# The aggregation's weights and lane numbers are read from PSUM instead of SBUF

## The chip, the cores and the metric

The kernel runs on one core of a Trainium2 chip. The metric is the device time of one execution in microseconds (us). A difference in a row of the profile is in us too, unless it is marked ns. The engines are TensorE (PE; its weight loads are listed as PEld), VectorE (DVE), ScalarE (ACT), GpSimd (POOL) and SyncE (SP).

## What is computed

A graph layer over 2500 nodes with 512 channels and 40000 edges sorted by destination, followed by a token-mixing branch and a gated MLP. Two attention layers over the edges come first, and they hold the part that is changed:

```python
for l in range(L):                                   # L = 2
    q = (x @ Wq[l] + bq[l]).reshape(N, H, D)         # N = 2500, H = 8, D = 64
    k = (x @ Wk[l] + bk[l]).reshape(N, H, D)
    v = (x @ Wv[l] + bv[l]).reshape(N, H, D)
    a = (q[dst] * k[src]).sum(-1) * scale
    ...                                              # softmax of a over the edges of one dst
    agg = jax.ops.segment_sum(alpha[:, :, None] * v[src], dst, num_segments=N).reshape(N, C)
    x = agg + (x @ Ws[l] + bs[l]) + enc
```

The changed stage is the `segment_sum`: for each edge the row `v[src]` is fetched, multiplied by the edge's eight head weights, and added into the row of its destination node.

## The kernel before

The edges lie in 336 slots of 128 (SLOTS; one edge per partition). Each slot belongs to one tile of 128 destination nodes. Each layer runs, one block after the other with a barrier between them: `project_nodes` (q, k, v), `score_edges`, `soften` (the softmax), `aggregate` and `combine`. Nothing of one block overlaps the next.

`score_edges` and `aggregate` both fetch rows with `gather` (L761): GpSimd issues one indirect DMA per slot, 128 rows of 2 KB, into a ring of U = 16 buffers. Before gather s it waits until VectorE has used the buffer of slot s - 16. GpSimd does nothing else in either block.

In `aggregate` VectorE works per slot, in this order: the one-hot `hot` (L1068), which compares the row of lane numbers `T["lane"]` (0 to 127, 128x128 f32) with the edge's local node number, a per-partition scalar; every fourth slot the copy of four slots' weights into the last eight columns of `wv` (L1075); then it waits for the slot's rows to land and writes the product `wv = vbuf * wt` (L1078), with the eight weights spread over 64 channels each. `wt` holds the weights of eight slots, copied from `weights` by the staging instruction (L1056) every eight slots. `wv` is a ring of R = 8 slots and `hot` one of 16. Before the rings come round VectorE waits for TensorE (`summed`).

TensorE multiplies `hot` by `wv` into the accumulator `psA` (L1118): two f32 matmuls per slot, 256 and 264 columns, which stand in the trace as four matmul records. Every four slots its queue loads the numbers of the node tiles (L767). ScalarE moves a full accumulator to `agg` (L1093) and clears it (L1095), 20 times per layer. SP loads `x` from `base_rows`, 20 transfers of 256 KB per layer.

In `score_edges` the corresponding product (L829) is `psQ[i] * kbuf[u]`: one operand comes from PSUM and the other from SBUF. Its one-hots (L808) are bf16, from SBUF to SBUF. Each slot's gather is of the same size as in `aggregate`.

Of the kernel before, what the change touches and what calls it, by code (L numbers as in the profile page):

```python
# [14 lines left out]
P = 128  # L15
# [3 lines left out]
H = 8  # L19
# [12 lines left out]
U = 16  # L32
# [60 lines left out]
def one(ap):  # L93

    return ap.rearrange("p o c -> p (o c)")
# [10 lines left out]
def turns(engine, n, body):  # L106


    body(0)
    with engine.Fori(1, n) as t:  # L110
        body(t)
# [10 lines left out]
def later(t):  # L122

    return not isinstance(t, int) or t > 0
# [629 lines left out]
def gather(pool, T, bufs, table, landed, freed, started):  # L754

    for s in range(SLOTS):
        if s >= U:

            pool.wait_ge(freed, s - U + 1)
            pool.sem_inc(started, 1)  # L760
        pool.indirect_dma_start(bufs[:, s % U, :], None, table,  # L761
                                bass.IndirectOffsetOnAxis(ap=T["src"][:, s:s + 1], axis=0)).then_inc(landed[s % U], 16)


def node_tiles(nc, engine, T, slot, n):

    return nc.values_load_multi_w_load_instructions(T["tile_of"][0:1, bass.ds(slot, n)], engines=[engine.engine],  # L767
                                                    min_val=0, max_val=NT - 1)[1]
# [243 lines left out]
def aggregate(nc, a, T, layer, v_dram, weights, agg, base_dram, x):  # L1012

    with ExitStack() as stack:
        m = Memory(nc, stack, f"agg{layer}")
        h, B, R = U // 2, 4, 8
        vbuf = m.sb("vbuf", [P, U, C])
        hot = m.sb("hot", [P, U, P])  # L1020
        wt = m.sb("wt", [P, 2, h, H])
        wv = m.sb("wv", [P, R, AW])
        zeros = m.sb("zeros", [P, 2, C // 2 + H])
        psA = m.ps("psA", [P, 2, 2, C])
        landed = [m.sem(f"landed{u}") for u in range(U)]
        hots, staged, beside, weighted, summed, blank, evicted, kept, started = (
            m.sem(x) for x in ("hots", "staged", "beside", "weighted", "summed", "blank", "evicted",
                               "kept", "started"))
        base_in = m.sem("base_in")
        local = T["local"]  # L1030
        parts = ((0, C // 2), (C // 2, AW))
        with nc.Block() as block:
            @block.sync
            def _(sp):
                def tile(t):
                    if later(t):

                        sp.wait_ge(weighted, t * U)
                    sp.dma_start(one(x[:, bass.ds(t, 1), :]), base_dram[bass.ds(t * P, P), :]).then_inc(base_in, 16)
                turns(sp, NT, tile)  # L1040
                sp.wait_ge(base_in, 16 * NT)

            @block.gpsimd
            def _(pool):
                gather(pool, T, vbuf, v_dram, landed, weighted, started)

            @block.vector
            def _(vec):
                vec.memset(zeros[:], 0.0).then_inc(blank, 1)

                def stage(t, half):
                    if later(t):

                        vec.wait_ge(weighted, (t - 1) * U + half * h + h)
                        vec.wait_ge(beside, (t - 1) * (U // B) + (half * h + h) // B)
                    vec.tensor_scalar(wt[:, half].rearrange("p u h -> p (u h)"),  # L1056
                                      weights[:, bass.ds((t * U + half * h) * H, h * H)],
                                      1.0, None, ALU.mult).then_inc(staged, 1)
                    vec.wait_ge(staged, t * 2 + half + 1)

                def turn(t):
                    for u in range(U):
                        if u % h == 0:
                            stage(t, u // h)
                        if later(t):

                            vec.wait_ge(summed, t * U + u + 2 - U)
                        vec.tensor_scalar(hot[:, u, :], T["lane"][:], local[:, bass.ds(t * U + u, 1)], None,  # L1068
                                          ALU.is_equal).then_inc(hots, 1)
                        if u % B == 0:  # L1070
                            if later(t) or u >= R:


                                vec.wait_ge(summed, t * U + u + B + 1 - R)
                            vec.tensor_scalar(wv[:, u % R:u % R + B, C:AW], wt[:, u // h, u % h:u % h + B, :], 1.0, None,  # L1075
                                              ALU.mult).then_inc(beside, 1)
                        vec.wait_ge(landed[u], t * 16 + 16)
                        vec.tensor_tensor(wv[:, u % R, 0:C].rearrange("p (h d) -> p h d", h=H),  # L1078
                                          vbuf[:, u, :].rearrange("p (h d) -> p h d", h=H),
                                          wt[:, u // h, u % h, :].unsqueeze(2).to_broadcast([P, H, D]),  # L1080
                                          ALU.mult).then_inc(weighted, 1)
                turns(vec, TURNS, turn)

            @block.scalar
            def _(act):
                act.wait_ge(blank, 1)
                act.sem_inc(evicted, 2)
                for d in range(NT):
                    full = act.value_load(T["full_at"][0:1, d:d + 1], min_val=1, max_val=SLOTS + 1)

                    act.wait_ge(summed, full if d < NT - 1 else SLOTS + 1)
                    for e, (lo, hi) in enumerate(parts):
                        act.copy(agg[:, d, lo:hi], psA[:, d % 2, e, 0:hi - lo]).then_inc(kept, 1)  # L1093
                    act.wait_ge(kept, 2 * d + 2)
                    act.copy(psA[:, d % 2, :, 0:C // 2 + H], zeros[:]).then_inc(evicted, 1)  # L1095

            @block.tensor
            def _(pe):
                pe.wait_ge(blank, 1)

                for bank in range(2):
                    for e in range(2):
                        last = pe.matmul(psA[:, bank, e, 0:C // 2 + H], T["ident"][:], zeros[:, e, :], start=True,
                                         stop=True)
                last.then_inc(summed, 1)

                def turn(t):
                    for u in range(U):
                        if u % B == 0:
                            tiles = node_tiles(nc, pe, T, t * U + u, B)  # L1110
                        d = tiles[u % B]
                        pe.wait_ge(hots, t * U + u + 1)
                        pe.wait_ge(beside, t * (U // B) + u // B + 1)
                        pe.wait_ge(weighted, t * U + u + 1)

                        pe.wait_ge(evicted, d + 1)
                        for e, (lo, hi) in enumerate(parts):
                            last = pe.matmul(psA[:, bass.ds(d % 2, 1), e, 0:hi - lo].rearrange("p o w -> p (o w)"),  # L1118
                                             hot[:, u, :], wv[:, u % R, lo:hi], start=False, stop=True,
                                             skip_group_check=True)  # L1120
                        last.then_inc(summed, 1)
                turns(pe, TURNS, turn)
# [1124 lines left out]
```

## Time and profile before

| | us |
|---|---|
| median of 3 runs | 3659.98 |
| lowest, highest | 3658.13, 3666.35 |
| the profiled execution, its own time | 3664.16 |
| its span | 3662.4 |

| engine | busy us | share of the span | instructions |
|---|---|---|---|
| PE | 2651.1 | 72% | 11106 |
| DVE | 2418.7 | 66% | 4726 |
| POOL | 1825.7 | 50% | 1645 |
| ACT | 1285.6 | 35% | 6512 |

The rows further down come from this one profiled execution. A row of a group of instructions gives, after the count, the busy time in us, the mean duration in ns, then the idle time of the engine just before them and what ended most of it. A row of the timeline begins with the start and the duration in us; what stands in brackets at its end is the idle time before it and what ended it. "issue" means that the profile shows nothing that was waited for. A timeline row with x3 merges three instructions that follow each other, and its duration covers them all. The two aggregations run from 810 to 1284 us and from 2035 to 2512 us of the span.

### The profile page before, as it was taken

How to read it: one execution, taken by the hardware profiler on the slowest of the kernel's cores; microseconds unless marked ns; L12 is line 12 of the kernel's file. 1: busy time of each engine (PE TensorE's matmuls, PEld its weight loads, DVE VectorE, ACT ScalarE, POOL GpSimd, SP SyncE). 2: the span in 40 equal slices, each digit the busy share in tenths (PEclk: the TensorE clock that was granted, in tenths of full speed). 3: DMA queues.
4: the chain of work that ended last, by engine and by line, in shares of the span. 5: the costliest groups of instructions: out<-in, count | busy, mean ns of one | idle time of the engine just before them, and what ended most of it. 6: DMA issues, size and time to landing. Idle time of an engine off the chain costs nothing. (4 is left out here: it accounts for less than half of the span.)

```text
span 3662.4 us, 54563 instructions
## 1 busy us (share of the span) xinstructions
PE 2651.1 (72%) x11106; PEld 1804.8 (49%) x11107; DVE 2418.7 (66%) x4726; ACT 1285.6 (35%) x6512; POOL 1825.7 (50%) x1645
## 2 busy tenths in 40 slices
PE   1898766757777749966665677773577988189998
PEld 1786333325555538832332455552465766167776
DVE  6555888876666655588888666667443454765555
ACT  0101988840000010078887000001332221454444
POOL 0012777737777701167775577776002343444444
PEclk8899899879999979999998899997798999589999
DMA  3433777737766743367775577663303231310100
GB/s 120 159 116 118 210 209 209 209 105 201 202 199 200 190 169 115 109 188 209 209 209 156 149 200 206 197 198 100 104 12 115 92 115 56 118 35 35 35 34 34
DMA packets 195463, 517.07 MB, mean 141 GB/s; under 512 B 29817, under 2 KB 30691, under 8 KB 195375
## 3 DMA queue, kind: packets, MB, share of 16 engines
q0 software_dynamic: 107520, 352.41, 33.9%
q1 hardware_dynamic: 76334, 142.71, 11.4%
q10 hardware_dynamic: 11520, 20.98, 1.5%
q8 instruction: 31, 0.51, 0.1%
q14 instruction: 58, 0.47, 0.0%
HBM read 453.19 MB, written 62.79 MB: 141 GB/s over the span
## 5 line engine op out<-in xcount | busy, mean ns | idle before, releaser
L761 POOL DMA_INDIRECT agg_vbuf<-v_rows,edges_src x672 | 730.9, 1088 | 297.9 <-issue 188.0
L1118 PE MATMUL agg_psA<-agg_wv,agg_hot 128*128 128x264 f32 (+1 forms) x2688 | 704.1, 406 | 236.2 <-DVE agg_hot L1068 99.4
L761 POOL DMA_INDIRECT score_kbuf<-k_rows,edges_src x672 | 637.8, 949 | 256.8 <-issue 161.6
L1118 PEld LDWEIGHTS agg_psA<-agg_wv,agg_hot 128*128 128x128 f32 x2688 | 490.1, 194 | 450.9 <-issue 392.1
L865 PE MATMUL score_psQ<-layer_q_parts,score_hotT 128*128 x2016 | 532.8, 420 | 196.5 <-DVE score_prod L829 143.5
L885 ACT ACTIVATE score_prod<-score_prod 128x64 f32<-128x64 f32 x2688 | 644.2, 243 | 54.4 <-DVE score_prod L829 54.0
L1078 DVE TENSOR_TENSOR agg_wv<-agg_vbuf,agg_wt 128x512 f32<-128x512 f32 x672 | 465.4, 692 | 290.6 <-DMA agg_vbuf<-v_rows,edges_src 288.5
L885 ACT ACTIVATION_READ_ACCUMULATOR score_prod<-score_prod 128x1 f32 x2688 | 506.5, 188 | 0.0
L829 DVE TENSOR_TENSOR score_prod<-score_psQ,score_kbuf 128x512 f32<-128x512 f32 x672 | 438.9, 685 | 92.5 <-DMA score_kbuf<-k_rows,edges_src 70.7
L102 PE MATMUL proj_psP<-proj_w,proj_xT 128*128 128x512 f32 x1920 | 454.8, 396 | 18.6 <-DVE proj_xT L703 9.2
L865 PEld LDWEIGHTS score_psQ<-layer_q_parts,score_hotT 128*128 128x128 bf16 x2016 | 211.3, 105 | 455.4 <-issue 305.1
L102 PEld LDWEIGHTS proj_psP<-proj_w,proj_xT 128*128 128x128 f32 x1920 | 362.5, 191 | 96.7 <-DVE proj_xT L703 10.0
L1093 ACT COPY layer_agg<-agg_psA 128x256 f32<-128x256 f32 x80 | 26.1, 378 | 910.3 <-PE agg_psA L1118 910.3
L750 POOL TENSOR_TENSOR proj_enc<-proj_enc,proj_bias 128x512 f32<-128x512 f32 x40 | 51.2, 1292 | 513.4 <-DMA proj_enc<-xn_rows 513.1
L2119 POOL TENSOR_TENSOR ffn_sums<-ffn_sums 128x512 f32<-128x512 f32 x110 | 173.0, 1572 | 212.7 <-DVE ffn_sums L2149 212.7
L1068 DVE TENSOR_SCALAR agg_hot<-kept_lane,edges_local 128x128 f32<-128x128 f32 x672 | 200.7, 299 | 18.8 <-DVE agg_wt L1056 13.8
L834 DVE TENSOR_REDUCE score_found<-score_prod 128x16 f32<-128x1024 f32 x168 | 203.0, 1208 | 0.0
L729 DVE TENSOR_TENSOR proj_out<-proj_psP,proj_bias 128x512 f32<-128x512 f32 x120 | 82.6, 691 | 171.3 <-PE proj_psP L102 170.9
L102 PE MATMUL ffn_psO<-kept_downT,ffn_hT 128*128 128x512 f32 x660 | 171.0, 422 | 25.7 <-DVE ffn_hT L2177 25.7
L2088 ACT ACTIVATE ffn_sums<-ffn_psP,kept_means 128x512 f32<-128x512 f32 x220 | 139.6, 685 | 82.9 <-PE ffn_psP L2047 80.9
L2149 DVE SCALAR_TENSOR_TENSOR ffn_sums<-ffn_psP,kept_means,ffn_sums 128x512 f32<-128x512 f32 x220 | 154.3, 741 | 18.7 <-PE ffn_psP L2047 18.6
L102 PEld LDWEIGHTS ffn_psO<-kept_downT,ffn_hT 128*128 128x128 f32 x660 | 133.2, 204 | 59.4 <-issue 15.8
(273 smaller groups left out, 3216.8 us busy)
## 6 DMA issues: line engine op xcount, KB each, us to landing
score_kbuf<-k_rows,edges_src POOLq DMA_INDIRECT x672, 3.7
agg_vbuf<-v_rows,edges_src POOLq DMA_INDIRECT x672, 3.8
proj_enc<-xn_rows SPq DMA_DIRECT2D x40, 256.0 KB, 3.1
base_rows<-proj_enc SPq DMA_DIRECT2D x40, 256.0 KB, 2.0
k_rows<-proj_out ACTq DMA_DIRECT2D x40, 256.0 KB, 2.1
v_rows<-proj_out ACTq DMA_DIRECT2D x40, 256.0 KB, 2.1
layer_x<-base_rows SPq DMA_DIRECT2D x40, 256.0 KB
xn_rows<-index_x SPq DMA_DIRECT2D x5, 1024.0 KB, 4.3
```

Of the source, the lines that this page charges most:

```text
L102: last = pe.matmul(out, left[i], right[j], start=start and n == 0, stop=stop and n == 2)
L761: pool.indirect_dma_start(bufs[:, s % U, :], None, table, bass.IndirectOffsetOnAxis(ap=T["src"][:, s:s + 1], axis=0)).then_inc(landed[s % ...
L829: vec.tensor_tensor(prod[:, j, i, :], psQ[i][:], kbuf[:, u, :], ALU.mult).then_inc(multiplied, 1)
L834: vec.tensor_reduce(found[:, j], prod[:, j, 0:V].rearrange("p i (h d) -> p i h d", h=H), AX.X, ALU.add).then_inc(reduced, 1)
L865: last = pe.matmul(psQ[i][:], hotT[:, j % 2, i, :], one(qp[:, k, bass.ds(d, 1), :]), start=(k == 0), stop=(k == 2))
L885: act.activation(at, at, ACT.Copy, accum_out=found_act[:, j, i - V, head:head + 1]).then_inc(reduced_act, 1)
L1068: vec.tensor_scalar(hot[:, u, :], T["lane"][:], local[:, bass.ds(t * U + u, 1)], None, ALU.is_equal).then_inc(hots, 1)
L1078: vec.tensor_tensor(wv[:, u % R, 0:C].rearrange("p (h d) -> p h d", h=H), vbuf[:, u, :].rearrange("p (h d) -> p h d", h=H), wt[:, u // h, ...
L1118: last = pe.matmul(psA[:, bass.ds(d % 2, 1), e, 0:hi - lo].rearrange("p o w -> p (o w)"), hot[:, u, :], wv[:, u % R, lo:hi], start=False, ...
L2088: act.activation(sums[:, f % 2, j, k, :], psP[k][:], ACT.Copy, scale=W["means"][:, j, f * KC + k:f * KC + k + 1]).then_inc(scaled, 1)
L2119: pool.tensor_tensor(sums[:, f % 2, j, 0, :], sums[:, f % 2, j, 0, :], sums[:, f % 2, j, 1, :], ALU.add).then_inc(summed, 1)
L2149: vec.scalar_tensor_tensor(out=half, in0=psP[k][:], scalar=W["means"][:, j, f * KC + k:f * KC + k + 1], in1=half, op0=ALU.mult, op1=ALU.ad ...
```

## The change

`wt` is allocated in PSUM instead of SBUF. A second PSUM tensor `lane` is added, and VectorE copies `T["lane"]` into it once per aggregation, with a wait for that copy. The one-hot reads `lane` from PSUM, the product and the copy of the weights into `wv` read `wt` from PSUM, and the staging instruction writes there. `vbuf`, `hot`, `wv` and `weights` stay in SBUF. In the built program `wt` lies in PSUM bank 0, `lane` in bank 1 and `psA` in banks 2 to 5; before, `psA` alone was there.

```diff
-        wt = m.sb("wt", [P, 2, h, H])
+        wt = m.ps("wt", [P, 2, h, H])
+        lane = m.ps("lane", [P, P])
...
-        base_in = m.sem("base_in")
+        base_in, laned = m.sem("base_in"), m.sem("laned")
...
                 vec.memset(zeros[:], 0.0).then_inc(blank, 1)
+                vec.tensor_copy(lane[:], T["lane"][:]).then_inc(laned, 1)
+                vec.wait_ge(laned, 1)
...
-                        vec.tensor_scalar(hot[:, u, :], T["lane"][:], local[:, bass.ds(t * U + u, 1)], None,
+                        vec.tensor_scalar(hot[:, u, :], lane[:], local[:, bass.ds(t * U + u, 1)], None,
                                           ALU.is_equal).then_inc(hots, 1)
```

The order of VectorE's instructions at the start of an aggregation, before the change (kept_lane is `T["lane"]`, edges_local the local node numbers):

```order
L1049 MEMSET agg_zeros 128x528
L1056 TENSOR_SCALAR agg_wt<-layer_weights 128x64
L1068 TENSOR_SCALAR agg_hot<-kept_lane,edges_local 128x128
L1075 TENSOR_SCALAR agg_wv<-agg_wt 128x4x8
L1078 TENSOR_TENSOR agg_wv<-agg_vbuf,agg_wt 128x512
```

The same place with the change; all lines behind the two new ones are three higher:

```order
L1050 MEMSET agg_zeros 128x528
L1051 COPY agg_lane<-kept_lane 128x128
L1059 TENSOR_SCALAR agg_wt<-layer_weights 128x64
L1071 TENSOR_SCALAR agg_hot<-agg_lane,edges_local 128x128
L1078 TENSOR_SCALAR agg_wv<-agg_wt 128x4x8
L1081 TENSOR_TENSOR agg_wv<-agg_vbuf,agg_wt 128x512
```

One copy is new at the head of each aggregation. Nothing else moves on any engine.

## Rows read from the trace of the kernel before

**Rows 1.** The page, costliest groups: gathers, VectorE's products and the one-hot.
```profile
L761 POOL DMA_INDIRECT agg_vbuf<-v_rows,edges_src x672 | 730.9, 1088 | 297.9 <-issue 188.0
...
L761 POOL DMA_INDIRECT score_kbuf<-k_rows,edges_src x672 | 637.8, 949 | 256.8 <-issue 161.6
...
L1078 DVE TENSOR_TENSOR agg_wv<-agg_vbuf,agg_wt 128x512 f32<-128x512 f32 x672 | 465.4, 692 | 290.6 <-DMA agg_vbuf<-v_rows,edges_src 288.5
...
L829 DVE TENSOR_TENSOR score_prod<-score_psQ,score_kbuf 128x512 f32<-128x512 f32 x672 | 438.9, 685 | 92.5 <-DMA score_kbuf<-k_rows,edges_src 70.7
...
L1068 DVE TENSOR_SCALAR agg_hot<-kept_lane,edges_local 128x128 f32<-128x128 f32 x672 | 200.7, 299 | 18.8 <-DVE agg_wt L1056 13.8
```

**Rows 2.** Table by stretch: PE, PEld, DVE, ACT, POOL busy, clock, DMA share, GB/s.
```profile
400.00:700.00 300.00, 212.94 (x960) 92.25 (x960) 264.36 (x554) 267.03 (x1993) 227.10 (x240) 0.90 0.73 209
810.49:1276.13 465.64, 350.58 (x1333) 244.62 (x1334) 314.29 (x792) 23.87 (x57) 363.55 (x335) 0.97 0.70 199
2036.04:2503.61 467.57, 349.55 (x1333) 242.64 (x1334) 313.65 (x791) 23.87 (x57) 365.45 (x335) 0.98 0.70 198
```

**Rows 3.** Who waited for whom, 810.49 to 1276.13: total us, times, longest.
```profile
DVE agg_wv L1078 <- DMA agg_vbuf<-v_rows,edges_src: 140.4, 264, 3.2
POOL agg_vbuf L761 <- issue: 91.7, 301, 0.3
...
POOL agg_vbuf L761 <- DVE agg_wv L1078: 10.1, 33, 0.3
```

**Rows 4.** Instructions of line 761: duration in ns, min/median/max.
```profile
L761 POOL DMA_INDIRECT score_kbuf<-k_rows,edges_src x672: 942/949/1127, 342.8 to 1988.0; - x168
L761 POOL DMA_INDIRECT agg_vbuf<-v_rows,edges_src x672: 942/1077/1447, 810.5 to 2503.6; - x168
```

**Rows 5.** Timeline of POOL in the first aggregation, three gathers.
```profile
861.42 0.94 POOL L761 DMA_INDIRECT agg_vbuf<-v_rows,edges_src  x1 [0.30 <-issue]
...
865.17 1.43 POOL L761 DMA_INDIRECT agg_vbuf<-v_rows,edges_src  x1 [0.30 <-issue]
...
868.29 0.94 POOL L761 DMA_INDIRECT agg_vbuf<-v_rows,edges_src  x1 [0.30 <-DVE agg_wv L1078]
```

**Rows 6.** Timeline of VectorE beside those three gathers.
```profile
861.72 0.69 DVE L1078 TENSOR_TENSOR agg_wv<-agg_vbuf,agg_wt 128x512 f32<-128x512 f32 x1 [1.23 <-DMA agg_vbuf<-v_rows,edges_src]
...
865.09 0.69 DVE L1078 TENSOR_TENSOR agg_wv<-agg_vbuf,agg_wt 128x512 f32<-128x512 f32 x1 [0.17 <-DMA agg_vbuf<-v_rows,edges_src]
...
868.14 0.19 DVE L1056 TENSOR_SCALAR agg_wt<-layer_weights 128x64 f32 x1
868.55 0.28 DVE L1068 TENSOR_SCALAR agg_hot<-kept_lane,edges_local 128x128 f32<-128x128 f32 x1 [0.23 <-PE agg_psA L1118]
```

**Rows 7.** Timeline of POOL in the first scoring block; 16 gather intervals from first to last.
```profile
419.41 0.95 POOL L761 DMA_INDIRECT score_kbuf<-k_rows,edges_src  x1 [0.30 <-DVE score_prod L829]
...
434.46 0.95 POOL L761 DMA_INDIRECT score_kbuf<-k_rows,edges_src  x1 [0.30 <-issue]
...
439.47 0.95 POOL L761 DMA_INDIRECT score_kbuf<-k_rows,edges_src  x1 [0.30 <-DVE score_prod L829]
```

**Rows 8.** Timeline of VectorE in the scoring block, three products in a row.
```profile
433.25 2.01 DVE L829 TENSOR_TENSOR score_prod<-score_psQ,score_kbuf 128x512 f32<-128x512 f32 x3
```

**Rows 9.** Timeline of POOL: first and last gather of each aggregation.
```profile
810.49 0.95 POOL L761 DMA_INDIRECT agg_vbuf<-v_rows,edges_src  x1 [46.63 <-POOLq L65]
...
1276.13 0.95 POOL L761 DMA_INDIRECT agg_vbuf<-v_rows,edges_src  x1 [0.30 <-issue]
...
2036.04 0.95 POOL L761 DMA_INDIRECT agg_vbuf<-v_rows,edges_src  x1 [47.10 <-POOLq L65]
...
2503.61 0.95 POOL L761 DMA_INDIRECT agg_vbuf<-v_rows,edges_src  x1 [0.30 <-issue]
```

**Rows 10.** Timeline of PE in the first aggregation: four slots in one row.
```profile
933.03 3.77 PE L1118 MATMUL agg_psA<-agg_wv,agg_hot 128*128 128x256 f32 x16 [0.43 <-issue]
```

**Rows 11.** VectorE's groups by shape: 336 columns from PSUM, then from SBUF.
```profile
L494 DVE TENSOR_SCALAR index_tile_of<-index_psd 128x336 f32<-128x336 f32 x1 | 0.5, 507 | 2.8 <-PE index_pss L566 2.8
...
L518 DVE TENSOR_SCALAR index_okh<-edges_local 128x336 f32<-128x336 f32 x1 | 0.3, 326 | 0.0
```

## The prediction, made before the changed kernel ran

> **What bounds the kernel now.** The change touches only the two aggregations, so I read those stretches and not the shares of the whole span. The table by stretch comes first [rows 2]: in 465.64 us the first aggregation issues 335 gathers. No engine is full (TensorE 350.58 us busy, VectorE 314.29, GpSimd 363.55), the DMA engines are 70% busy, and so the waits must say who sets the pace. They do [rows 3]: VectorE waits 140.4 us for rows to land. GpSimd waits for VectorE in 33 places only, each time for the same 0.3 us that it takes between any two gathers (91.7 us in 301 places), so those 33 are no real waits. GpSimd never pauses beyond that. The chain is thus: a gather takes 1.09 us, 0.30 us pass, the next begins; everybody else follows. 465.64 / 335 = 1.390 us per slot, and 467.57 / 335 = 1.396 in the second layer [rows 9].
>
> The next thing to see is that the same instruction is faster elsewhere. In the scoring blocks it takes 949 ns on average, in the aggregations 1088 [rows 1]; the minimum is 942 in both, but the medians are 949 and 1077, and the longest is 1447 in the aggregations [rows 4]. Same rows, same size, same table layout. Something in the aggregation holds it back.
>
> The timeline shows what [rows 5, 6]. Three gathers:
> - The one at 865.17 takes 1.43 us. A product had begun at 865.09 and ran to 865.78, that is 0.61 us into the gather. 1.43 - 0.945 = 0.485 us of lengthening: what was left of the product, less about 0.12 us.
> - The one at 861.42 takes 0.94 us. Here a product also runs beside it, but it began at 861.72, after the gather had started.
> - The one at 868.29 takes 0.94 us. Beside its start run the staging instruction (868.14 to 868.33) and, inside it, the one-hot at 868.55. Neither lengthens it.
>
> So a gather is held when a product is already running shortly after the gather starts, until that product ends. The last question is which products do this. In the scoring block three products run without a gap from 433.25 to 435.26, and the gather at 434.46 starts in the middle of them with 0.80 us of product still to come; it takes 0.95 us [rows 7, 8]. By the law above it would have taken about 1.6. The two products have the same shape and nearly the same duration, 692 and 685 ns [rows 1]. They differ in this: the aggregation's reads two operands from SBUF, the scoring's one from PSUM and one from SBUF.
>
> Here a page of the Trainium skill bears on the case, and one half of it speaks against the change. SBUF — State Buffer, section "Who interferes with whom", says that a VectorE instruction with two SBUF inputs contends with a GpSimd instruction that reads SBUF, because the second input comes through a read interface shared with GpSimd. The rows at 865.17 and 434.46 agree with that. The same section then infers that such a product does not stall DMAs issued by GpSimd, since generating descriptors needs the write interface; by that inference the gathers would gain nothing and the sum below would be 0. The 1.43 us of the gather at 865.17 speak against it.
>
> **The change, part by part.**
>
> *The product reads one operand from SBUF.* It becomes like the scoring's. The gathers should take what they take there. The interval between gathers there is (439.47 - 419.41) / 16 = 1.254 us [rows 7]; over a longer stretch it is 300 / 240 = 1.250 [rows 2]. The two aggregations have 335 intervals each: 465.64 + 467.57 = 933.21 us now [rows 9], 670 x 1.254 = 840.2 after. The term is -93.0 us; with 1.250 it is -95.7. The cause that ends last is then still the gather. I take 1.254, since it is from gathers that follow each other without a disturbance.
>
> *The price of the product itself.* From 692 to something like the 685 of L829, which also has a PSUM operand. 0 on the path.
>
> *The one-hot from PSUM.* No row shows this instruction with a PSUM source. The nearest are 336 columns at 507 ns from PSUM and 326 from SBUF [rows 11], 181 ns more, so 128 / 336 of it, an estimate of 69 ns per slot. Upper bound: all 181 ns. Lower bound: nothing, if its SBUF form gains nothing now. It happens between products and is covered while VectorE still waits for rows. VectorE is busy 314.29 / 335 = 0.938 us per slot [rows 2]; 0.938 + 0.069 = 1.01, with the upper bound 1.12, and the slot will last 1.254. The cover holds; without it each 0.1 us would cost 67 us. The copy of weights into `wv` and the staging instruction are a quarter and an eighth of an instruction per slot; if each took 0.1 us longer that would be 0.04 us per slot, within the same cover.
>
> *The copy of the lane numbers and its wait.* Twice, some 0.3 us. Behind the wait stand the staging instruction, the first one-hot and the first product. The first product waits for its rows in any case, 3.2 us, the longest of those waits [rows 3]. Price 0.
>
> *What is late next.* TensorE: four slots in a row take 3.77 us, and between two such rows 0.43 us pass when work is waiting [rows 10], together 4.20 / 4 = 1.05 us per slot. With its slow moments it is 350.58 / 335 = 1.047 busy plus 0.11, or 1.15. Under 1.254, by 8%. The granted clock is 0.97 and 0.98 in the aggregations and 0.90 in the scoring block [rows 2]; TensorE will be busier per us than now, and at 0.90 the 1.047 becomes 1.13 and the sum 1.24. That is close, and I keep it for the range. The DMA engines: a gather moves 0.262 MB, in the scoring block at 209 GB/s with 73% share; the aggregation adds 20 loads of `x`, now 199 GB/s in all, then 199 x 1.390 / 1.254 = 221 GB/s and 0.70 x 1.108 = 78%. A ring of 16 buffers covers slower landings.
>
> The sum: -93 + 0 + 0 + 0. The profiled execution took 3664.16 us, so 3571.1 after. It stood 4.2 above the median of the runs, 3659.98; against the median the time is 3567.
>
> **The rivals.**
>
> *TensorE or VectorE takes the bound over.* For it: TensorE's floor of 1.15 to 1.24 lies close to 1.254, and every stall of a few us must be made up from little slack. Against it: the rings let VectorE run up to four to eight slots ahead of it. At 1.29 us per slot the gain is 933.2 - 864.3 = 69 us: 3591. At 1.32 it is 49 us: 3611.
>
> *The gathers are not released.* What differs between the products is not only the memory: the aggregation's spreads eight weights over 64 channels each, and this stays. If that pattern holds the gather, nothing changes: 3660. The inference quoted from the Trainium skill gives the same time. For it: the trace has no spread operand in PSUM. Against it: nothing in the rows ties the hold to the pattern, and the spread operand is the smaller of the two in memory.
>
> *Slower.* The spread operand is read slowly from PSUM, beside TensorE's writes there, and VectorE becomes the bound. It decides from 1.390 us per slot, that is if L1078 grows by more than 1.39 - 1.01 = 0.38 us, from 0.69 to 1.07. If each of the 512 elements took twice as long, the product would take about 1.2 us and a slot 1.52: 670 x 0.13 = 87 us more, 3747. Against it: 685 ns with a PSUM operand beside a TensorE that is busy 71% of the stretch [rows 1, 2].
>
> **How the numbers follow.** Gathers at the scoring block's interval: 0.85. Another engine takes over part of the gain: 0.08. Not released: 0.04. Slower: 0.03. About 0.2%, or 7 us, is what a measurement of this kernel can tell from no change. Faster 0.93, same 0.04, slower 0.03. The range: at the low end the interval of 1.250 (3564) and the spread of the runs around it, some 5 us below: 3559. At the high end half of the takeover case: 3591.
>
> **What would show each step right or wrong.** Right: in both aggregations the gathers have a median near 949 ns and a maximum below 1200, about 1.254 us apart, and the last gather of the first aggregation starts 420 us after its first. VectorE's waits for landings shrink but stay. The one-hot takes 0.07 us longer or less. The product stays at 0.69 us. The prediction is wrong if gathers still reach 1.4 us (the hold has another cause), if GpSimd shows real waits for VectorE (VectorE or TensorE is the bound), or if the product grows past 1 us.

## The result: 3567.6 us, 2.5% faster

| | us |
|---|---|
| before, median (runs from 3658.13 to 3666.35) | 3659.35 |
| changed kernel, median (runs from 3562.90 to 3569.16) | 3567.59 |
| ratio, with its 95% interval | 0.9746 (0.9734 to 0.9759) |
| profiled execution, before and after | 3664.16 and 3567.26 |
| its span, before and after | 3662.4 and 3565.6 |

The page of the changed kernel answers to [rows 1]. The gathers of the aggregation now take what those of the scoring block take:

```profile
L761 POOL DMA_INDIRECT agg_vbuf<-v_rows,edges_src x672 | 635.3, 945 | 298.7 <-issue 172.7
L761 POOL DMA_INDIRECT score_kbuf<-k_rows,edges_src x672 | 636.1, 947 | 257.1 <-issue 162.1
...
L1081 DVE TENSOR_TENSOR agg_wv<-agg_vbuf,agg_wt 128x512 f32<-128x512 f32 x672 | 460.6, 685 | 167.2 <-DMA agg_vbuf<-v_rows,edges_src 158.6
...
L1071 DVE TENSOR_SCALAR agg_hot<-agg_lane,edges_local 128x128 f32<-128x128 f32 x672 | 232.4, 346 | 18.6 <-DVE agg_wt L1059 12.7
```

The table of instructions of line 761 (duration in ns, min/median/max) and the table by stretch, both for the changed kernel, answer to [rows 4] and [rows 2]:

```profile
L761 POOL DMA_INDIRECT agg_vbuf<-v_rows,edges_src x672: 940/946/963, 811.1 to 2408.2; - x168
```

```profile
811.06:1229.87 418.81, 323.52 (x1332) 242.50 (x1332) 327.55 (x793) 23.86 (x57) 316.76 (x336) 0.99 0.76 221
1989.46:2408.20 418.74, 325.29 (x1332) 243.14 (x1332) 326.77 (x792) 23.86 (x57) 316.70 (x335) 0.99 0.75 221
```

The stretches run from the first gather to the last of each aggregation, as in [rows 9]. 418.81 + 418.74 = 837.55 us now, 933.21 before: 95.7 us less, out of the 96.8 us by which the span shrank. The whole gain is in the interval between gathers, 418.81 / 335 = 1.250 us instead of 1.390. The longest gather takes 963 ns where one of 1447 was [rows 4].

The timeline of the changed kernel shows the case that used to be expensive, a gather that starts while a product runs. GpSimd first, then VectorE:

```profile
862.34 0.95 POOL L761 DMA_INDIRECT agg_vbuf<-v_rows,edges_src  x1 [0.30 <-DVE agg_wv L1081]
```

```profile
862.15 0.68 DVE L1081 TENSOR_TENSOR agg_wv<-agg_vbuf,agg_wt 128x512 f32<-128x512 f32 x1
```

The product ran until 862.83, 0.49 us into the gather. By the law read from [rows 5, 6] the gather would have taken 0.945 + 0.49 - 0.12 = 1.32 us; it took 0.95.

The waits between 810 and 1240 us, in total us, times and longest, answer to [rows 3]:

```profile
POOL agg_vbuf L761 <- issue: 87.4, 287, 0.3
DVE agg_wv L1081 <- DMA agg_vbuf<-v_rows,edges_src: 80.0, 190, 2.6
...
POOL agg_vbuf L761 <- DVE agg_wv L1081: 14.6, 48, 0.3
```

This window reaches 10 us past the last gather; from the first gather to the last, the stretch of [rows 3], VectorE waits for landings 77.0 us in 186 places, where it was 140.4. GpSimd still pauses for 0.3 us only, whatever is named. So the gathers are still what ends last.

### The profile page after: what moved, and what is told of

It reads as the page before. It is cut to its first block and busy times, and to the rows that moved or that the text cites. A ratio compares the mean times of both kernels' runs of the same rounds, so it can differ in the third digit from the quotient of the medians.

```text
span 3565.6 us, 54565 instructions
## 1 busy us (share of the span) xinstructions
PE 2590.4 (73%) x11106; PEld 1799.1 (50%) x11107; DVE 2447.2 (69%) x4728; ACT 1285.7 (36%) x6512; POOL 1727.5 (48%) x1645
## 5 line engine op out<-in xcount | busy, mean ns | idle before, releaser
L1121 PE MATMUL agg_psA<-agg_wv,agg_hot 128*128 128x264 f32 (+1 forms) x2688 | 653.5, 394 | 193.7 <-DVE agg_hot L1071 134.8
L761 POOL DMA_INDIRECT agg_vbuf<-v_rows,edges_src x672 | 635.3, 945 | 298.7 <-issue 172.7
L865 PE MATMUL score_psQ<-layer_q_parts,score_hotT 128*128 x2016 | 523.7, 415 | 202.6 <-DVE score_prod L829 139.0
L1081 DVE TENSOR_TENSOR agg_wv<-agg_vbuf,agg_wt 128x512 f32<-128x512 f32 x672 | 460.6, 685 | 167.2 <-DMA agg_vbuf<-v_rows,edges_src 158.6
L1071 DVE TENSOR_SCALAR agg_hot<-agg_lane,edges_local 128x128 f32<-128x128 f32 x672 | 232.4, 346 | 18.6 <-DVE agg_wt L1059 12.7
L834 DVE TENSOR_REDUCE score_found<-score_prod 128x16 f32<-128x1024 f32 x168 | 203.0, 1209 | 0.0
```

The costliest lines, as they stand in the source:

```text
L761: pool.indirect_dma_start(bufs[:, s % U, :], None, table, bass.IndirectOffsetOnAxis(ap=T["src"][:, s:s + 1], axis=0)).then_inc(landed[s % ...
L834: vec.tensor_reduce(found[:, j], prod[:, j, 0:V].rearrange("p i (h d) -> p i h d", h=H), AX.X, ALU.add).then_inc(reduced, 1)
L865: last = pe.matmul(psQ[i][:], hotT[:, j % 2, i, :], one(qp[:, k, bass.ds(d, 1), :]), start=(k == 0), stop=(k == 2))
L1071: vec.tensor_scalar(hot[:, u, :], lane[:], local[:, bass.ds(t * U + u, 1)], None, ALU.is_equal).then_inc(hots, 1)
```

## The experiments

The formula that the prediction read from [rows 5, 6] is called the law below: a held gather takes 0.945 us plus what is left of the product at the gather's start, less 0.12 us; where less than that is left, nothing is added. **Theory A**: a gather is held by a VectorE product that reads two operands from SBUF, if the product is still running about 0.12 us after the gather's start, and until it ends. **Theory B**: the one-hot, whose operand moved as well, is what held the gathers. **Theory C**: the spread of eight weights over 64 channels held them, as an access pattern in SBUF.

### Each half of the change alone

The weights alone, made on the kernel before:

```diff
-        wt = m.sb("wt", [P, 2, h, H])
+        wt = m.ps("wt", [P, 2, h, H])
```

> Only the staged weights lie in PSUM; the one-hot still reads the lane numbers from SBUF. Theory A (a product that reads two operands from SBUF holds a gather that starts beside it): the whole gain is here, 3567 us, gathers in the aggregations at a median of 946 ns with no maximum above 1000, 1.25 us apart, and the one-hot back from 346 to about 280 to 300 ns. Theory B (the one-hot from SBUF holds the gathers): no gain, 3660 us, gathers at a median of 1077. If both share in it: between them.

Measured: 3565.55 us, ratio 0.9746 (0.973 to 0.9762), the same as the full change. The lane numbers alone, made on the changed kernel:

```diff
-        wt = m.ps("wt", [P, 2, h, H])
+        wt = m.sb("wt", [P, 2, h, H])
         lane = m.ps("lane", [P, P])
```

> Only the lane numbers lie in PSUM; the product reads both operands from SBUF. Theory A: 3660 us, gathers at a median near 1077 ns with a maximum above 1400, and the one-hot at 346 ns. Theory B: 3567 us, gathers at 946 ns. The slower one-hot by itself should cost nothing under either, since VectorE waits for rows in both kernels.

Measured: 3657.94 us, ratio 1.0 (0.999 to 1.0009). The instructions of line 761 in the two kernels, weights alone first:

```profile
L761 POOL DMA_INDIRECT agg_vbuf<-v_rows,edges_src x672: 942/946/1005, 809.6 to 2406.7; - x168
```

```profile
L761 POOL DMA_INDIRECT agg_vbuf<-v_rows,edges_src x672: 940/1066/1497, 811.7 to 2500.0; - x168
```

Theory B falls: all of the gain comes from the weights, and moving the lane numbers neither costs nor brings time that these runs could tell from nothing. Two expectations missed. The longest gather with the weights alone was to stay below 1000 ns and took 1005. And the one-hot was to take 280 to 300 ns, since it reads SBUF as before. Its rows, weights alone and lanes alone:

```profile
L1068 DVE TENSOR_SCALAR agg_hot<-kept_lane,edges_local x672: 272/310/527, 809.7 to 2411.5; 128x128 f32<-128x128 f32 x168
```

```profile
L1071 DVE TENSOR_SCALAR agg_hot<-agg_lane,edges_local x672: 336/345/352, 812.2 to 2504.3; 128x128 f32<-128x128 f32 x168
```

Reading SBUF, it takes 272 ns at best but up to 527, 347 on average; reading PSUM, it takes 345 nearly every time. When it begins decides. In the timeline of the kernel with the weights alone 158 one-hots begin 0.5 to 0.6 us after a gather's start; they take 380 to 493 ns and end on average 0.05 us after the gather does. The 59 that begin in a gather's first 0.4 us take 277 to 288 ns. The one-hots that read PSUM take 344 to 353 ns wherever they begin, in the changed kernel. So the second half of the change exchanges a quick but unsteady one-hot for a steady one with the same average, off the path in both.

### Half of the slots

Made on the changed kernel, with a second staging instruction into an SBUF tile `ws`:

```diff
+        ws = m.sb("ws", [P, 2, h, H])
...
-                                          wt[:, u // h, u % h, :].unsqueeze(2).to_broadcast([P, H, D]),
+                                          (ws if u % 2 else wt)[:, u // h, u % h, :].unsqueeze(2).to_broadcast([P, H, D]),
```

> The changed kernel, with the weights staged twice, in PSUM and in SBUF; the product of every even slot reads PSUM, that of every odd slot SBUF. Theory A: half of the products hold a gather, half do not, so half of the 92 us comes back: 3605 to 3620 us, mean duration of the aggregations' gathers about 1015 ns (half way between 945 and 1088), median near 950. A rival in which the hold depends on how busy VectorE is on the whole, not on which product it runs: the time stays near 3567 or near 3660.

Measured: 3626.67 us, ratio 0.9914 (0.9898 to 0.9931), gathers at a mean of 1031 ns and a median of 946. The timeline of this kernel, GpSimd and then VectorE, shows both kinds side by side:

```profile
896.02 1.17 POOL L761 DMA_INDIRECT agg_vbuf<-v_rows,edges_src  x1 [0.30 <-issue]
897.50 0.95 POOL L761 DMA_INDIRECT agg_vbuf<-v_rows,edges_src  x1 [0.30 <-issue]
898.75 1.27 POOL L761 DMA_INDIRECT agg_vbuf<-v_rows,edges_src  x1 [0.30 <-issue]
```

```profile
895.68 0.69 DVE L1083 TENSOR_TENSOR agg_wv<-agg_vbuf,agg_ws 128x512 f32<-128x512 f32 x1 [0.36 <-DMA agg_vbuf<-v_rows,edges_src]
...
897.27 0.69 DVE L1083 TENSOR_TENSOR agg_wv<-agg_vbuf,agg_wt 128x512 f32<-128x512 f32 x1 [0.64 <-DMA agg_vbuf<-v_rows,edges_src]
...
898.51 0.69 DVE L1083 TENSOR_TENSOR agg_wv<-agg_vbuf,agg_ws 128x512 f32<-128x512 f32 x1 [0.28 <-DMA agg_vbuf<-v_rows,edges_src]
```

All three gathers start while a product runs. The first product reads its weights from SBUF as well (`ws`) and ends 0.35 us into the gather: 0.945 + 0.35 - 0.12 = 1.175, measured 1.17. The third ends 0.45 us in: 1.275, measured 1.27. The second reads its weights from PSUM (`wt`), ends 0.46 us in, and its gather takes 0.95. Which product runs decides, not how busy VectorE is.

The size was off: 59 us came back, where 37 to 52 were expected (3605 to 3620). The gathers' mean of 1031 instead of 1015 accounts for it: (1.031 - 0.945) x 670 = 58 us. Per SBUF product the hold is 2 x 0.086 = 0.172 us here and 0.143 in the kernel before. The timelines show where the difference lies. Before, 524 of the 672 products were running when a gather started, and those gathers took 1126 ns on average. Here it was 226 of the 336 SBUF products, and the gathers took 1199. Fewer products meet the start of a gather, but those that do have more of their run left. When a product runs depends on when its rows were fetched, and so on the earlier holds; half of the products need not bring half of the hold. Why the two settle this way was not tested.

### Another pattern, two SBUF operands

Made on the kernel before:

```diff
-                        vec.tensor_tensor(wv[:, u % R, 0:C].rearrange("p (h d) -> p h d", h=H),
-                                          vbuf[:, u, :].rearrange("p (h d) -> p h d", h=H),
-                                          wt[:, u // h, u % h, :].unsqueeze(2).to_broadcast([P, H, D]),
+                        vec.tensor_tensor(wv[:, u % R, 0:C], vbuf[:, u, :], vbuf[:, u, :],
                                           ALU.mult).then_inc(weighted, 1)
```

> The kernel before, with the product computed as the fetched rows times themselves: two SBUF operands again, but none that spreads eight weights over 64 channels. The weights are left out of the product. Theory A: the hold stays, 3660 us, gathers in the aggregations at a mean of 1080 to 1100 ns and a maximum above 1400. Theory C (the spread operand from SBUF is what holds the gathers): 3567 us, gathers at 946 ns.

Measured in one execution: 3660.65 us. The instructions of line 761 of this kernel:

```profile
L761 POOL DMA_INDIRECT agg_vbuf<-v_rows,edges_src x672: 942/1072/1472, 810.6 to 2500.8; - x168
```

The hold is there in full without any spread operand. Theory C falls.

### The hold, brought into the scoring block

Made on the changed kernel:

```diff
-                            vec.tensor_tensor(prod[:, j, i, :], psQ[i][:], kbuf[:, u, :],
+                            vec.tensor_tensor(prod[:, j, i, :], kbuf[:, u, :], kbuf[:, u, :],
                                               ALU.mult).then_inc(multiplied, 1)
```

> The changed kernel, with the scoring block's product computed as the fetched rows times themselves: two SBUF operands where PSUM and SBUF were. The queries are left out of the product, though they are still computed. Theory A: the hold now appears in the two scoring blocks. Products run there for 0.61 us of each 1.25, about as in the aggregations, so the scoring gathers go from a mean of 947 to 1050 to 1120 ns and the time from 3567 to 3640 to 3690 us; the aggregations' gathers stay at 945. If the hold were a matter of the aggregation block (its table, its buffers, its one-hots), nothing changes: 3567.

Measured in one execution: 3662.44 us, 95 above the changed kernel's median and inside the expected range. The page's groups of this kernel, by shape:

```profile
L761 POOL DMA_INDIRECT score_kbuf<-k_rows,edges_src x672 | 736.9, 1097 | 257.0 <-issue 159.9 <-SPq L797 52.9 <-DVE score_prod L829 44.2
...
L761 POOL DMA_INDIRECT agg_vbuf<-v_rows,edges_src x672 | 635.2, 945 | 297.1 <-issue 176.3 <-POOLq L65 93.0 <-DVE agg_wv L1081 27.7
```

A block that had run freely is now held: 1097 ns on average against 947, while the aggregation's gathers stay at 945. The effect belongs to the pair of instructions and not to the aggregation. The mean is about that of the old aggregation (1088), but the spread is another: the median is 987 and the longest gather 2586 ns, where the aggregation had 1077 and 1447. In this block up to four products follow each other without a pause, and a hold lasts through all of them. GpSimd and then VectorE:

```profile
1604.69 2.59 POOL L761 DMA_INDIRECT score_kbuf<-k_rows,edges_src  x1 [0.30 <-DVE score_prod L829]
```

```profile
1603.96 2.49 DVE L829 TENSOR_TENSOR score_prod<-score_kbuf 128x512 f32<-128x512 f32 x4
```

The row of four products ends at 1606.45, 1.76 us into the gather: 0.945 + 1.76 - 0.12 = 2.585, measured 2.59. "Until it ends" in theory A means until the last of such a row ends.

### Another kind of instruction

Made on the changed kernel: a long instruction between SBUF tensors in every fourth slot. First a copy of 1024 columns (one input), then in its place a product of 512 columns (two inputs):

```diff
+                        if u % B == 2:
+                            if later(t) or u > B:
+                                vec.wait_ge(again, t * (U // B) + u // B)
+                            vec.tensor_scalar(spare[:], weights[:, 0:2 * C], 1.0, None, ALU.mult).then_inc(again, 1)
```

> The changed kernel with one more VectorE instruction in every fourth slot of the aggregation: a copy of 1024 f32 columns from SBUF to SBUF (one input), whose result nobody reads. It runs for about as long as a product, some 0.68 us. Open is whether a single-input instruction between SBUF tensors also holds a gather. Theory A in the narrow form (only an instruction with two SBUF inputs holds it): every gather stays between 940 and 1010 ns and the time at 3567 us. The wide form (any instruction that uses both of VectorE's SBUF ports holds it; the Trainium skill, SBUF — State Buffer, section Who interferes with whom, says so of copies in the two-port modes): up to a quarter of the gathers are lengthened, some to 1.4 us, and the time rises to 3580 to 3605 us.

```diff
-                            vec.tensor_scalar(spare[:], weights[:, 0:2 * C], 1.0, None, ALU.mult).then_inc(again, 1)
+                            vec.tensor_tensor(spare[:, 0:C], weights[:, 0:C], weights[:, C:2 * C], ALU.mult).then_inc(again, 1)
```

> The same with a product of two SBUF operands of 512 f32 columns in the place of the copy, 0.69 us too, in every fourth slot; its result is not read. Theory A, wide or narrow: some of the gathers beside it are held, up to 1.4 us, mean 960 to 1000 ns, and the time rises to 3580 to 3605 us. This is the yardstick for the copy: same place, same length, another kind.

Measured in one execution each: 3592.52 us with the copy, 3587.28 with the product, both in the range of 3580 to 3605. The copy holds the gathers too. GpSimd and VectorE in the kernel with the copy:

```profile
847.67 1.20 POOL L761 DMA_INDIRECT agg_vbuf<-v_rows,edges_src  x1 [0.30 <-issue]
```

```profile
847.37 0.68 DVE L1077 TENSOR_SCALAR agg_spare<-layer_weights 128x1024 f32<-128x1024 f32 x1
```

The copy ends 0.38 us into the gather: 0.945 + 0.38 - 0.12 = 1.205, measured 1.20. The kernel with the product follows the same law and shows the limit of it:

```profile
840.37 1.16 POOL L761 DMA_INDIRECT agg_vbuf<-v_rows,edges_src  x1 [0.30 <-issue]
...
850.75 0.95 POOL L761 DMA_INDIRECT agg_vbuf<-v_rows,edges_src  x1 [0.30 <-issue]
```

```profile
840.03 0.68 DVE L1077 TENSOR_TENSOR agg_spare<-layer_weights 128x512 f32<-128x512 f32 x1
...
850.15 0.68 DVE L1077 TENSOR_TENSOR agg_spare<-layer_weights 128x512 f32<-128x512 f32 x1
```

The product at 840.03 ends 0.34 us into its gather and costs it 0.21 us. The one at 850.15 ends 0.08 us in and costs nothing. The narrow form of theory A falls: two inputs are not needed.

A single input does not always hold a gather, though. In the scoring block VectorE runs a reduction of 1024 SBUF columns (L834), longer than any product. The kernel before, GpSimd and VectorE:

```profile
426.94 0.95 POOL L761 DMA_INDIRECT score_kbuf<-k_rows,edges_src  x1 [0.30 <-issue]
```

```profile
426.38 1.21 DVE L834 TENSOR_REDUCE score_found<-score_prod 128x16 f32<-128x1024 f32 x1
```

The reduction ends 0.65 us into the gather, which by the law would take 1.475 us; it takes 0.95. Of the 162 gathers of that trace that start with more than 0.125 us of a reduction to go, none takes more than 0.96 us. Nor do one-hots that read PSUM hold one: in the changed kernel 80 gathers start with as much of such a one-hot to go, and the longest takes 0.95 us. The copy moves 1024 columns in 0.68 us, the reduction in 1.21, and the product 512 in 0.68: the copy takes in about twice as many columns per us as the other two.

The Trainium skill (SBUF — State Buffer, section "Who interferes with whom") says that copies and `tensor_scalar` can run in modes that use two ports, and that, of such an instruction and one of GpSimd, the one that issues first blocks the other. The rows of the copy at 847.37, which had started first, agree.

The copy also shows a hold that the law does not cover. Four gathers of its kernel, 1193 to 1316 ns long, started without a copy; the copy began 0.39 to 0.52 us later. Each of them ended 0.12 us after the copy did. Here the gather had started first and was held all the same; by the starts alone the copy should have waited.

### Is the gather the bound now, and by how much?

Half of TensorE's work taken away, made on the changed kernel:

```diff
-                        for e, (lo, hi) in enumerate(parts):
+                        for e, (lo, hi) in list(enumerate(parts))[1:]:
                             last = pe.matmul(psA[:, bass.ds(d % 2, 1), e, 0:hi - lo].rearrange("p o w -> p (o w)"),
```

> The changed kernel without the first of the two matmuls per slot in the aggregation (the accumulation of the first 256 channels is left out). If the gathers set the pace of the aggregations now: no change, 3560 to 3570 us (a few us less at each end of the two blocks at most), gathers still 1.25 us apart. If TensorE limits a part of it: more than 10 us less.

Measured: 3568.28 us, ratio 0.9745 (0.9728 to 0.9763). No difference. And work added to VectorE:

```diff
                         vec.tensor_scalar(hot[:, u, :], lane[:], local[:, bass.ds(t * U + u, 1)], None,
                                           ALU.is_equal).then_inc(hots, 1)
+                        if later(t) or u >= 2:
+                            vec.wait_ge(again, t * U + u - 1)
+                        vec.tensor_scalar(spare[:, u % 2, :], lane[:], local[:, bass.ds(t * U + u, 1)], None,
+                                          ALU.is_equal).then_inc(again, 1)
```

> The changed kernel with a second one-hot from PSUM per slot, written into a buffer that nobody reads: 0.26 us more of VectorE per slot, more than the upper bound of 0.18 that the prediction gave to the one-hot's growth. If VectorE has that slack (0.95 us per slot where no wait is seen, plus 0.26 is 1.21, under 1.25): 3567 to 3575 us, and VectorE's waits for landings nearly gone. If it has not: at 1.30 us per slot, 34 us more, 3600.

Measured: 3564.16 us, ratio 0.9739 (0.9721 to 0.9757), 3 us under the expected range and within the spread of the runs. The first aggregation by stretch (columns as in [rows 2]), half the matmuls first, then the second one-hot:

```profile
813.06:1231.87 418.81, 289.18 (x670) 153.52 (x670) 327.08 (x792) 23.87 (x57) 316.75 (x335) 0.71 0.76 221
```

```profile
808.80:1227.50 418.70, 323.35 (x1332) 242.17 (x1332) 394.89 (x1123) 23.87 (x57) 316.72 (x335) 1.00 0.76 221
```

With half the matmuls and with 20% more VectorE time the stretch stays at 418.8 us. The gathers are the bound. VectorE is then 94% busy, and its waits for landings in both aggregations have gone from 158.6 to 28.8 us:

```profile
L1086 DVE TENSOR_TENSOR agg_wv<-agg_vbuf,agg_wt 128x512 f32<-128x512 f32 x672 | 458.5, 682 | 31.6 <-DMA agg_vbuf<-v_rows,edges_src 28.8
```

Per slot VectorE had 327.55 / 335 = 0.98 us of busy time and now has 1.18, so 0.20 us were added and 0.07 are left idle. VectorE's slack was larger than the upper bound that the prediction gave to the one-hot's growth (0.18), and it is nearly used up here. No kernel of this study is clearly below the changed one; the one with the weights alone reaches the same time with a single edit.

## Why the prediction was right

The forecast was 3567 us; 3567.6 was measured. By its steps:

- **The bound** [rows 2, 3]: right. The intervals between gathers made 95.7 of the 96.8 us of the span.
- **The law of the hold** [rows 5, 6]: right in the main, and it met four held gathers of other kernels to 0.01 us. It also holds beyond the three gathers that it was read from. In the kernel before, 500 gathers of the aggregations start while a product has more than 0.125 us to run, and 481 of them follow the law to 0.015 us. The other 19 are not held at all: their product had begun less than 0.05 us before the gather. So the product's start counts as well as its end, which the prediction did not see. Another reading was too quick. The gather at 868.29 was shown to stay free beside the staging instruction and the one-hot. But that staging instruction ended 0.04 us into the gather, before the 0.12 us from which a hold counts, and the one-hot began only after its start. Those rows could not show that single-input instructions between SBUF tensors are harmless, and the long copy showed that they are not, in that form. With the weights alone in PSUM the one-hots from SBUF left a trace of it, a longest gather of 1005 ns instead of 963. They are just too short to matter. The rows of before had a hint too: the longest gather of the scoring block took 1127 ns [rows 4], and it started beside a run of one-hots (L808) from SBUF to SBUF.
- **The comparison with the scoring block** [rows 7, 8]: right. It was the step that carried the forecast, since it showed the state after the change in the trace of before. Bringing the hold into the scoring block confirmed it from the other side.
- **The term of the sum**: -93.0 with an interval of 1.254; measured 1.250 and -95.7, which was the other end of the bound. The step that chose 1.254 cost 2.7 us. The difference of 4.2 us between the profiled execution and the median was carried over to the changed kernel, where the profiled execution stood at the median (3567.26 and 3567.59). By the medians the gain is 91.8 us. The two misses, 3.9 us too high in the profiled execution and 4.2 too much taken off, cancel. That the forecast came within 1 us is luck; that it came within the 8 us over which runs of one kernel spread is not.
- **The one-hot**: 69 ns more was the estimate. The medians went from 281 to 345 ns, 64 more, the means from 299 to 346, 47 more. Covered, as said, and so is another whole one-hot.
- **VectorE's load**: 1.01 us per slot was expected, 327.55 / 335 = 0.98 measured. **The DMA engines**: 221 GB/s and 78% expected, 221 and 76% measured.
- **TensorE**: its floor was put at 1.15, or 1.24 if the granted clock fell to 0.90 with more work per us. The clock did not fall, it rose from 0.97 to 0.99, and TensorE was busy for 323.52 / 335 = 0.97 us per slot instead of 1.05. This term only widened the range. That TensorE would be busier per us came true (77% of the stretch instead of 75%); that its clock might fall for it was the wrong direction.
- **The rival "not released"** rested on the spread operand. It is excluded by the kernel without one. The inference quoted from the Trainium skill (SBUF — State Buffer, "Who interferes with whom"), that a product with two SBUF inputs does not stall DMAs issued by GpSimd, is contradicted here by 92 us; what the page calls an inference, the measurement decides.

## What to carry to other kernels

When one instruction has two typical durations in two stages, compare what runs beside it, and at what moment: here the start and the end of a product relative to the start of a gather sorted all 500 gathers of the kernel before that met one. If GpSimd's gathers set the pace, look for long VectorE instructions beside them that read two operands from SBUF, or that copy from SBUF to SBUF as the long copy here did. One operand in PSUM was enough for the product. The reduction, and one-hots of 0.3 us, could stay. Price such a change from a stage that already works that way, and check the cover of what becomes slower.

## What the runs showed that was not expected

- A copy with a single SBUF input holds a gather as a product with two does, while the reduction with a single one does not. The 168 copies cost 25 us and the 168 products 20 (one execution each).
- The contention goes both ways. With the weights alone in PSUM, the one-hot from SBUF took up to 527 ns where its shortest was 272. In the kernel before, 19 products began less than 0.05 us before a gather; they took 0.75 us instead of 0.69, and the gather took no longer. Rows of one such pair stand below. The border is not sharp: in the kernels with the lanes alone and with the plain pattern, 9 gathers whose product began that late were held all the same.
- The granted TensorE clock of the aggregation fell to 0.71 when half of its matmuls were left out (289.18 us busy of 418.81), and stood at 0.99 with all of them (323.52 us busy). These are means over the stretch of its two levels, 1.2 and 2.4 GHz: at 0.99 it was almost always the upper one, at 0.71 it was a mixture. So TensorE's busy time did not fall by half with its work. The clock alone would make 323.52 / 2 x 0.99 / 0.71 = 226 us of it; why 289 were busy stays open. As TensorE was not the bound, the time did not change.

A product that began 0.04 us before a gather and left it alone, in the kernel before (GpSimd, VectorE):

```profile
814.25 0.94 POOL L761 DMA_INDIRECT agg_vbuf<-v_rows,edges_src  x1 [0.30 <-issue]
```

```profile
814.21 0.76 DVE L1078 TENSOR_TENSOR agg_wv<-agg_vbuf,agg_wt 128x512 f32<-128x512 f32 x1 [3.24 <-DMA agg_vbuf<-v_rows,edges_src]
```
